# Graph network kernel: destination one-hots and the first key expansion in one stage, layer loop turned, edge messages in PSUM

## The reference, cut to what matters

```python
gate = silu(edge_attr @ F1W + F1b) @ F2W + F2b
gate = gate + (emb[atom_z[src]] * (emb[atom_z[dst]] @ adapt)).sum(-1, keepdims=True)
cw = where(distances < 6, 0.5 * (cos(pi * distances / 6) + 1.0), 0.0)
mj = node_mult[dst]
msg = gate * h[dst] * (cw * mj)[:, None]
agg, tot = segment_sum(msg, src), clip(segment_sum(mj, src), 1e-08)
h = _ln(h + agg / tot[:, None], gn, bn)
for i in range(4):
    Q, K = _ln(h @ Wq[i], gq[i], bq[i]), _ln(h @ Wk[i], gk[i], bk[i])
    score = (Q[src] * K[dst]).sum(-1) + 0.1 * (edge_attr * Q[src][:, :40]).sum(-1) + logm[dst]
    ...
```

## Time and profile before

| what | value |
|---|---|
| median of 3 runs | 15879.01 us (15866.77 to 15881.79) |
| the profiled execution | 15882.66 us |
| its span | 15880.9 us |
| busy in the span | PE 55%, PEld 46%, DVE 71%, ACT 33%, POOL 56% |
| mean granted clock of PE | 0.748 of full speed |

### The profile page before, as it was taken

One profiled execution on the slowest core, in us unless ns is written; L12 is line 12 of the kernel. 1 busy time (PEld: TensorE's weight loads), 2 busy tenths in 40 slices (PEclk: granted clock), 3 DMA queues, 4 the chain that ended last, 5 costly groups with the idle time before them and its releaser, 6 DMA issues. The chain is left out here.

```text
span 15880.9 us, 387212 instructions
## 1 busy us (share of the span) xinstructions
PE 8773.5 (55%) x112803; PEld 7285.1 (46%) x112803; DVE 11264.9 (71%) x28016; ACT 5196.8 (33%) x15610; POOL 8967.8 (56%) x11086
## 2 busy tenths in 40 slices
PE   2011015555543479957995799489926666544342
PEld 1011003333331168846884788478814444343332
DVE  6986017787866669976997799779845544369788
ACT  0000002222220036624662466246613333323222
POOL 6787777777766434413441344144437777637365
PEclk9855555666665599969996999699957778785765
DMA  3523346666672276627662766276612222162543
GB/s 110 196 77 103 103 100 112 114 115 115 115 93 52 39 252 177 176 57 254 176 176 71 240 176 176 87 226 176 161 36 64 67 64 64 48 209 77 141 126 57
DMA packets 1458768, 1976.72 MB, mean 124 GB/s; under 512 B 412088, under 2 KB 1125944, under 8 KB 1451645
## 3 DMA queue, kind: packets, MB, share of 16 engines
q1 hardware_dynamic: 1073394, 1326.44, 26.6%
q0 software_dynamic: 309216, 511.82, 19.0%
q10 hardware_dynamic: 75960, 136.18, 2.7%
HBM read 1245.76 MB, written 614.07 MB: 117 GB/s over the span
## 5 line engine op out<-in xcount | busy, mean ns | idle before, releaser
L684 POOL DMA_INDIRECT attend_rows<-key_rows,attend_fetch_now x1824 | 1754.7, 962 | 2024.0 <-PE attend_seg L1820 1696.8
L1864 ACT ACTIVATE attend_hot<-attend_lane_hot,attend_share 128x128 f32<-128x128 fp8e4 x7296 | 2228.6, 388 | 1238.0 <-DVE attend_share L1887 967.8
L684 POOL DMA_INDIRECT edges_rows<-raw,edges_perm_now x1824 | 1856.6, 1018 | 636.8 <-issue 624.5
L684 POOL DMA_INDIRECT keys_rows<-table,keys_staged x1564 | 1653.3, 1057 | 470.9 <-issue 470.9
L1820 PE MATMUL attend_seg<-attend_rows,attend_hot 128*128 128x49 f32 x14592 | 1809.4, 278 | 136.1 <-ACT parts_layer L1868 62.3
L1820 PEld LDWEIGHTS attend_seg<-attend_rows,attend_hot 128*128 128x128 f32 x14592 | 1725.7, 194 | 228.8 <-issue 228.3
L684 POOL DMA_INDIRECT mlp_xin<-table,mlp_staged x1564 | 1514.7, 968 | 472.7 <-issue 469.5
L1807 PE MATMUL attend_qx<-attend_table,attend_oht 128*128 128x90 bf16 x21888 | 1087.9, 207 | 72.1 <-DMA attend_oht<-src_hots 70.8
L1904 DVE TENSOR_REDUCE attend_mraw<-attend_top 128x2 f32<-128x1024 f32 x912 | 1110.6, 1218 | 8.4 <-PE attend_top L1840 8.3
L1631 POOL COPY expand_table<-k 128x156 bf16 x912 | 291.3, 319 | 1355.2 <-issue 663.1
L684 POOL DMA_INDIRECT tally_rows<-rows_by_source,tally_origin_now x912 | 883.6, 969 | 299.6 <-issue 234.1
(11 more groups left out here) (545 smaller groups left out, 22544.6 us busy)
## 6 DMA issues: line engine op xcount, KB each, us to landing
key_rows<-expand_out SPq DMA_DIRECT2D x304, 624.0 KB
attend_ea<-edge_attrs SPq DMA_DIRECT2D x912, 160.0 KB
attend_table<-q SPq DMA_DIRECT2D x1832, 67.5 KB
expand_oht<-dst_hots SPq DMA_DIRECT2D x304, 384.0 KB, 3.9
attend_oht<-src_hots SPq DMA_DIRECT2D x912, 128.0 KB
attend_lane_hot<-src_hots_by_edge SPq DMA_DIRECT2D x912, 128.0 KB
raw<-keys_rows ACTq DMA_DIRECT2D x46, 2176.0 KB
rows_by_source<-spread_out SPq DMA_DIRECT2D x152, 576.0 KB, 4.8
```

What stands on the lines that cost most here:

```text
L684: return nc.gpsimd.indirect_dma_start(out=out, out_offset=None, in_=table, in_offset=bass.IndirectOffsetOnAxis(ap=index, axis=0))
L1864: ins = nc.scalar.activation(hot[p][:, u, c, :], lane_hot8[r][:, u, c, :], ACT.Copy, scale=share[p][:, u, c:c + 1])
```

## The change

1. `edge_pass`: `val`, `gate` and `rest` lie in PSUM (`rest` in the bank of `gate`). The copy of the gate by ACT and that of the lanes into `k.sloc` are gone. DVE adds the type term directly to the product in PSUM, the window's sum and first product are one instruction, its last product (`faded`) lies in PSUM, and the message is `(ps_2 + wgt) * (x * faded)`.
2. `hots_and_first` becomes three parts. `first_nodes` does the scans, the copies and the layer norm, while POOL gathers the lanes of chunks 0 to 16 into `k.lanes`, which now outlives the stage. The table stage of layer 0 does the same with chunks 17 to 36. `hots_and_expand` spreads, compares and stores the one-hots and does layer 0's expansion from the one-hots in SBUF, while POOL gathers chunks 37 to 113.
3. The layer loop is turned: three times attend, combine, update, next tables, expand; then a last attend, combine and update written out behind it.

```diff
+EARLY_A, EARLY_B = 17, 37
 # edge_pass
-        val, rest = ph.sb("val", [P, COL, RW]), ph.sb("rest", [P, COL, RW])
+        numbers_and_near = ph.ps("numbers", [P, 512])
+        numbers, faded = numbers_and_near[:, 0:P], numbers_and_near[:, P:P + COL]
+        val = ph.ps("val", [P, 512])[:, 0:COL * RW].rearrange("p (c w) -> p c w", w=RW)
+        gate_and_rest = ph.ps("gate", [P, 512])
...
-                    act.wait_ge(s_2, n - 1)
-                    a(gate[p][:], ps_2[:, 0:COL * F].rearrange("p (c f) -> p c f", f=F), ACT.Copy).then_inc(s_2c, 1)
...
-                    ch.step(v.tensor_copy(k.sloc[:, bass.ds(n * COL, COL)], r[:, :, SL]))
...
-                    ch.done(v.tensor_scalar(cw[o][:], cw[o][:], 1.0, None, ALU.add))
-                    ch.step(v.tensor_tensor(cw[o][:], cw[o][:], near[o][:], ALU.mult))
-                    dve.wait_ge(s_2c, n)
-                    ch.done(v.tensor_tensor(gate[o][:], gate[o][:], bc(wgt[:], F), ALU.add))
-                    ch.step(v.tensor_tensor(cw[o][:], cw[o][:], r[:, :, MU], ALU.mult))
-                    ch.step(v.tensor_tensor(gate[o][:], gate[o][:], r[:, :, X:X + F], ALU.mult))
+                    ch.done(v.scalar_tensor_tensor(out=cw[o][:], in0=cw[o][:], scalar=1.0, in1=near[o][:], op0=ALU.add, op1=ALU.mult))
+                    ch.step(v.tensor_tensor(faded, cw[o][:], r[:, :, MU], ALU.mult))
+                    dve.wait_ge(s_2, n)
+                    v.tensor_tensor(gate, ps_2[:, 0:COL * F].rearrange("p (c f) -> p c f", f=F), bc(wgt[:], F), ALU.add).then_inc(s_2c, 1)
+                    ch.wait()
+                    ch.step(v.tensor_tensor(scaled[:], r[:, :, X:X + F], bc(faded, F), ALU.mult))
...
-                    ch.done(v.tensor_tensor(val[:, :, 0:F], gate[o][:], bc(cw[o][:], F), ALU.mult))
+                    dve.wait_ge(s_2c, n)
+                    ch.done(v.tensor_tensor(val[:, :, 0:F], gate, scaled[:], ALU.mult))
 # hots_and_expand: SP, for each chunk n
+            for n in range(CHN):
+                if done <= n + 3 < CHN:
+                    put(n + 3)
+                if n + 2 < CHN:
+                    load(n + 2)
+                sp.wait_ge(s_eq, (n + 2) * HCH)
+                sp.dma_start(k.oht_d.rearrange("(p u) w -> p u w", p=P)[:, n * HCH:(n + 1) * HCH, :], oht[n % 2][:]).then_inc(s_kept[n % 2], 16)
+                if n >= 1:
+                    store(n - 1)
 # PE, then DVE
+            with pe.Fori(0, LOOPS) as t:
+                for b in two:
+                    for u in tiles:
+                        spread_lanes(t * 2 + b + 2, b, u, t + 1)
+                        rows_out(t * 2 + b + 1, 1 - b, u)
...
+            with dve.Fori(0, LOOPS) as t:
+                for b in two:
+                    dve.wait_ge(s_kept[b], (t + 1) * 16)
+                    dve.wait_ge(s_stored[1 - b], (t + 1 + b) * 16)
+                    for u in tiles:
+                        compare(t * 2 + b + 2, b, u)
+                        evict(t * 2 + b + 1, 1 - b, u)
 # program
-                hots_and_first(nc, k, i)
+                first_nodes(nc, k, i, range(0, EARLY_A))
...
+                layer_tables(nc, k, i, 0, range(EARLY_A, EARLY_B))
+                hots_and_expand(nc, k, EARLY_B)
+            with nc.Fori(0, LAYERS - 1) as layer:
+                with nc.sbuf_tensor("parts_layer", [P, NS * SUMS], F32) as k.parts:
+                    attend(nc, k, "attend")
+                    combine(nc, k, SUMS, True, "collect_layer", k.keep_u, k.erow)
+                layer_update(nc, k, i, layer, "update")
+                with nc.sbuf_tensor("k3", [P, 3, NT * KROW], BF16) as k.k3:
+                    layer_tables(nc, k, i, layer + 1)
+                    expand(nc, k)
...
```

More of the change, by code:

```diff
@@ L1248, in _, with lanes_at, gather_lanes, store_lanes @@
             dve.wait_ge(s_ev, CHN)
-def hots_and_first(nc, k, i):
-    HALF, WIDTH = NS // (2 * HCH), F + 2
+def lanes_at(k, n):
+    return k.dloc_b.rearrange("(u p) c -> p u c", p=P)[:, n * HCH:(n + 1) * HCH, :], k.lanes[:, n * HCH:(n + 1) * HCH, :]
+def gather_lanes(nc, pool, k, chunks, s_got):
+    for m, n in enumerate(chunks):
+        if m >= 2:
+            pool.wait_ge(s_got[m % 2], (16 * HCH) * (m // 2))
+        for u in range(n * HCH, (n + 1) * HCH):
+            gather(nc, k.lanes[:, u, :], k.dloc_a, k.origin[:, u:u + 1]).then_inc(s_got[m % 2], 16)
+def store_lanes(sp, k, chunks, s_got, s_put):
+    for m, n in enumerate(chunks):
+        sp.wait_ge(s_got[m % 2], (16 * HCH) * (m // 2 + 1))
+        into, kept = lanes_at(k, n)
+        sp.dma_start(into, kept).then_inc(s_put, 16)
+    sp.wait_ge(s_put, 16 * len(chunks))
+def first_nodes(nc, k, i, chunks):
+    WIDTH = F + 2
     with ExitStack() as ctx:
-        ph = Phase(nc, ctx, "hots")
+        ph = Phase(nc, ctx, "first")
         norm = Norm(ph)
@@ L1258, in hots_and_first, with _, hots_and_expand @@
         tot, t1 = ph.sb("tot", [P, NT]), ph.sb("t1", [P, NT, F])
-        s_step, s_w = ph.sem("s_step"), ph.sem("s_w")
+        s_step, s_w, s_put = ph.sem("s_step"), ph.sem("s_w"), ph.sem("s_put")
+        s_got = [ph.sem(f"s_got{b}") for b in range(2)]
         parts = k.parts[:, 0:NS * WIDTH].rearrange("p (u w) -> p u w", w=WIDTH)
-        two = range(2)
+        block = ph.block()
+        @block.gpsimd
+        def _(pool):
+            gather_lanes(nc, pool, k, chunks, s_got)
+        @block.sync
+        def _(sp):
+            sp.dma_start(gain[:], i["L0_gnn_gn"].partition_broadcast(P)).then_inc(s_w, 16)
+            sp.dma_start(bias[:], i["L0_gnn_bn"].partition_broadcast(P)).then_inc(s_w, 16)
+            store_lanes(sp, k, chunks, s_got, s_put)
+        @block.scalar
+        def _(act):
+            norm.act(act)
+        @block.vector
+        def _(dve):
+            v = nc.vector
+            ch = Chain(dve, s_step)
+            for f in range(WIDTH):
+                ch.step(v.tensor_tensor_scan(parts[:, :, f], k.keep_u[:], parts[:, :, f], 0.0, ALU.mult, ALU.add))
+            ch.wait()
+            for t in range(NT):
+                at = dve.value_load(k.erow[0:1, t:t + 1], min_val=0, max_val=NS - 1)
+                ch.step(v.tensor_copy(k.agg[:, t, 0:WIDTH], k.parts[:, bass.ds(at * WIDTH, WIDTH)]))
+            ch.wait()
+            ch.step(v.tensor_copy(k.count[1][:], k.agg[:, :, F + 1]))
+            ch.done(v.tensor_scalar(tot[:], k.agg[:, :, F], 1e-8, None, ALU.max))
+            ch.done(v.reciprocal(tot[:], tot[:]))
+            ch.done(v.tensor_tensor(t1[:], k.agg[:, :, 0:F], bc(tot[:], F), ALU.mult))
+            ch.done(v.tensor_tensor(t1[:], t1[:], k.h[:], ALU.add))
+            dve.wait_ge(s_w, 32)
+            norm.dve(dve, ch, t1[:], k.h[:], gain[:], bias[:])
+def hots_and_expand(nc, k, done):
+    CHN = NS // HCH
+    LOOPS = CHN // 2 - 1
+    with ExitStack() as ctx:
+        ph = Phase(nc, ctx, "hots")
+        two, tiles = range(2), range(HCH)
         row = [ph.sb(f"row{b}", [1, HCH, W], BF16) for b in two]
@@ L1366, in combine @@
+            dve.wait_ge(s_stored[1], (LOOPS + 1) * 16)
+            for u in tiles:
+                evict(CHN - 1, 1, u)
 def combine(nc, k, width, softmax, tag, keep_u, erow):
```

211 lines of the change are left out of this document (109 added, 102 removed).

## The result

| | before | changed |
|---|---|---|
| median | 15880.4 us (4 runs) | 15611.26 us (4 runs, 15591.82 to 15622.2) |
| the profiled execution | 15882.66 us | 15621.44 us |
| its span | 15880.9 us | 15619.8 us |

The account below looks back on a forecast made before the run. DVE's chain was taken to bound the edge pass (42 us less), POOL's gathers the one-hot stage; 119 + 118 + 507 = 744 for 1017, 273 less. Together 315 less: 15564 us, own range 15500 to 15630.

Parts of the forecast that it names:

- DVE's chain as the bound: Edge pass: DVE's chain, not POOL's gathers, sets the period; 0.20 us less a chunk, 42 us in 208 chunks.
- short instructions follow each other by 0.08 us, so that is what goes: Edge pass: dropping the lanes copy into `k.sloc`, which overlaps its neighbours, saves 0.08 us a chunk.
- Rival A: Edge pass: gathers, not DVE, set it; 0.58 us a chunk, 120 us less instead of 42, total 15486; chance 0.15.
- Rival C: Edge pass: casts from PSUM lengthen DVE's chain, 0.2 us a chunk, 42 us more instead of less, total 15648; chance 0.12.
- 146 us of POOL: first_nodes: POOL's need if each scan held a gather up for its whole 1.1 us, 27 us more than the 119.
- my 91 us: first_nodes: POOL's 68 gathers at 1.343 us, taken as covered by DVE's 119 us.
- A spread 0.47 us at a granted clock of 0.50 and 12 products at 0.040, 0.48 us: Combined stage: PE's time for a tile, 0.95 us together, as much as DVE's.
- the 497 of the stores: Combined stage: the stores' landing as latest of four rates, 4.36 us a chunk for 114 chunks; 507 us with the ends.
- 4.95 us in my sum: Combined stage: landing of one-hots and key rows, 4.0 us for 384 KB plus 0.96 for 288 KB more.
- The sign I had named for PE's clock: Combined stage: DVE's waits being on PE instead of for stores would show PE's clock as the failed step.
- Rival B: Combined stage: stores land in time and DVE sets it, 440 us, total 15497; chance 0.12.
- Rival D: Combined stage: PE and DVE work in turn, 2.36 us a tile, 1076 us, total 16143, slower; chance 0.04.

Follow-up runs that it names:

- short_only: Kernel before with only the edge pass's short-instruction edits (lanes copy dropped, window's sum and first product fused): period 10.43 us against 10.65, ratio 0.9984.
- psum_only: Changed kernel with the edge pass's lanes copy and two window instructions back, message, gate and rest still in PSUM: period 10.70 us, ratio 0.9904.
- changed_no_puts: Changed kernel without the lanes' writes to DRAM in the combined stage, so later one-hots are of other lanes: stage 542.2 us, ratio 0.9797.
- earlier_no_puts: lanes_earlier without the lanes' writes to DRAM in the combined stage, so later one-hots are of other lanes: stage 449.7 us, ratio 0.9756.
- three_buffers: Changed kernel with three instead of two buffers of lanes, one-hots, key tables and key rows in the combined stage: stage 557.0 us, ratio 0.9807.
- lanes_earlier: Changed kernel with three buffers, spread over 128 partitions, lanes written six chunks ahead instead of three, rows loaded three ahead: stage 528.1 us, ratio 0.9803.
- changed_again: The changed kernel itself, unedited, on the same chip as the others as a mark: stage 578.1 us, period 10.29 us, ratio 0.9825.
- spread_128_rows: Changed kernel with the lanes' spread as a product over 128 partitions instead of one, two buffers kept: stage 551.0 us, ratio 0.9832.

## Why the prediction was right or wrong

**The edge pass: the right bound, one term short.** I took DVE's chain as the bound; the run with more work for DVE confirms it for the changed kernel. For the kernel before it is not shown: short_only took some 0.4 us of small instructions out of DVE's chain, and the period fell by 0.22. From one instruction's start to the next, mean over some 195 chunks of the timeline (lines of the kernel before):

| part of DVE's chain | before, us | changed, us | difference | predicted |
|---|---|---|---|---|
| list, lanes, copy (L1180, L1193, L1195) | 0.71 | 0.43 | -0.28 | -0.08 |
| window (L1221, L1222) | 0.38 | 0.19 | -0.18 | -0.24 |
| type term (L1224) | 0.59 | 0.47 | -0.12 | -0.12 |
| L1231 | 0.30 | 0.20 | -0.10 | -0.10 |
| two casts (L878, L880) | 0.85 | 1.22 | +0.36 | +0.39 |
| all else | 7.85 | 7.79 | -0.06 | -0.05 |
| chain | 10.68 | 10.30 | -0.38 | -0.20 |

The step that failed is "short instructions follow each other by 0.08 us, so that is what goes": 0.28 us went in the first row. The copy into `k.sloc` takes its address from a register, and an instruction of DVE's sequencer that works on registers stands between the wait for the lanes' cast and the copy. Behind the same wait the next instruction has none. From psum_only, which has the copy back, its register instruction and the copy; then, from the changed kernel, the instruction that follows the cast there:

```profile
L1198 DVEq FUSED_REGOPS  x152: 57/69/69, 2328.6 to 4489.4; - x152
...
3006.77 0.17 DVE L1198 COPY edges_sloc<-edges_rows 128x8 f32 x1 [0.23 <-DVE edges_sl L1196]
```

```profile
3014.94 0.17 DVE L1198 TENSOR_SCALAR edges_near<-edges_rows 128x8 f32<-128x8 f32 x1 [0.16 <-DVE edges_sl L1195]
```

At the mean, DVE is idle behind the cast for 0.24 us in the kernel before, 0.25 in psum_only, and 0.15 in the changed kernel. So 0.08 of the missing 0.20 us is the place of the copy's register instruction; 0.08 is a shorter cast (254 ns before, 175 changed), which fits with fewer long gathers beside it, and 0.03 is L1180. psum_only, with gathers at 955 ns, shows 0.55 us from the start of the cast to the instruction behind the copy, and the changed kernel 0.33: there the copy is nearly all of it. 0.36 us in 208 chunks are 75 us, the 74 measured, within what the pass varies by.

Rival A (POOL sets the pass) was not the case, but is less than 0.2 us away. Rival C, and the rule on PSUM operands of the Trainium skill (VectorE: DVE Perf Modes, "Why PSUM operands drop a tier"), had the casts right (575 ns, 565 expected; from 208 to 336 elements the rows give 1.02 ns for each, not 1.04, which moves the sum by 1 ns); the small instructions outweighed them, and the edge pass of psum_only, which has the casts without them, is not faster than before.

**first_nodes and the tables: right.** 121.0 and 116.7 us for 119 and 118. For the gathers under the scans I had feared 146 us of POOL; they took 114, and the 1.343 us a gather that my 91 us rested on did not hold there.

**The combined stage: two terms mis-sized, and their order wrong.** "A spread 0.47 us at a granted clock of 0.50 and 12 products at 0.040, 0.48 us": the first came from a stage at 0.50, the second from the expansion, whose clock was 0.92. Two rows at different clocks were added. At 0.50 the products take 0.64 and the tile 1.166 us, not 0.95, so PE stood at 532 us, above the 497 of the stores that I held to be the latest. And the stores' landing, 4.95 us in my sum, was 6.6 at the median of the 50 chunks that waited for it (from the issue of a buffer's key rows to DVE's start behind the wait for them); in changed_no_puts only 7 chunks waited. The 4.95 rested on a landing of 4.0 us for 384 KB, which is a load of one-hots in the expansion and not a store, in a stage without 8-byte writes. I had counted the writes' issue on SP and not their time in the DMA engines. Without them the stage is 542 us, PE's 532 and its ends. The sign I had named for PE's clock, DVE waiting for PE, would have misled: it shows 16 us of such waits against 98 for stores.

Rival B (DVE sets the stage, 440 us) is what earlier_no_puts shows, at 450, once all three other bounds are gone. Rival D did not come: PE ran ahead. By the prediction's own mark, a stage over 560 us, the forecast is wrong. That the total still came near is partly luck: the edge pass gave 32 us more than the sum had, and the stage 79 less.

**The loop turned: no difference to be seen.** What lies behind took 10048 us before and 10054 after; across the ten further kernels built on the changed one it was 10027 to 10078, without order, and 10098 in short_only, which has the old loop.

**Better versions.** No kernel that computes everything beat the changed one by much: three_buffers and lanes_earlier have ratios of 0.9807 and 0.9803 against 0.9825 and 0.983, 29 to 43 us, with intervals that overlap. For lanes_earlier there is a closer comparison: it ran on the same chip as changed_again, with a median of 15561.5 us against 15595.1, and all its five runs (up to 15567.8) lie below all four of the other (from 15592.8). The next 78 us are in the writes of the lanes.

## What to carry to other kernels

Take the durations of one engine's pieces from stretches with the same granted clock, and ask which clock the merged stage will have. When stages are merged, count small transfers by their packets: they cost time in the DMA engines that the large stores beside them need. Where two engines have the same period, an edit that frees one pays only if the other has room; try both halves of a change apart before crediting either.

## What was not expected of the hardware

With the spread as a product over one partition the granted clock stayed down, however busy PE was. In three_buffers PE was busy for 100 of 100 us (4990 to 5090) at 0.50; in spread_128_rows the same columns over 128 partitions, zeros but for one, ran at 1.00 in the same stretch, with PE busy for 70. The Trainium skill (TensorE: Matmul & The Clock Gate, "What's actually happening") says that the clock follows how busy PE has been; by busy time as the profile counts it these rows do not agree, and the measurement decides.

Beside a scan with two SBUF inputs a gather's issue takes 1.69 us instead of 0.94, and then keeps step with every second scan.

In all kernels the stage has a slow stretch where POOL's last 40 or so gathers run, 6.5 instead of 5.2 us a chunk in changed_again, and 5.4 instead of 4.67 even without the writes. Its cause was not tried.
